# A charge for two narrow token-attention steps in a row in a list schedule, with new priorities, in a macaron layer on one core

## What is computed

```python
x = x + 0.5 * ffn(layernorm(x), ...)
x = x + attn(layernorm(x), ...)
x = x + 0.5 * ffn(layernorm(x), ...)

def ffn(x, ...):                      # per token
    h = rmsnorm(x, gamma1)
    q = (h @ Wq + bq).reshape(b, t, 16, 16)
    kv = ((h @ Wdown + bdown) @ Wup + bup).reshape(b, t, 16, 32)
    k, v = split(kv, 2)
    att = softmax(einsum('bthd,btgd->bthg', q, k) / 4)   # over the heads of ONE token
    out = einsum('bthg,btgd->bthd', att, v).reshape(b, t, 256)
    x = x + (out @ Wo + bo)
    h2 = rmsnorm(x, gamma2)
    gate = softmax(h2 @ Wg + bg)                         # 8 experts
    return x + einsum('btd,edf,bte->btf', h2, We, gate)

def attn(x, ...):                     # 8 groups of 32 features
    scores = einsum('bngh,bmgh->bnmg', q, k) / 16
    probs = softmax(scores, axis=-1)  # over the groups g
    return einsum('bnmg,bmgh->bngh', probs, v)
```

## Time and profile before

| | |
|---|---|
| Median of 3 runs | 992.51 us (992.35 to 993.81) |
| Profiled execution | 993.92 us, span 991.8 us, 28114 instructions |
| PE busy | 953.0 us (96%) |
| PEld busy | 755.2 us (76%) |
| DVE busy | 854.7 us (86%) |
| POOL busy | 792.7 us (80%) |
| ACT busy | 642.2 us (65%) |
| Granted TensorE clock | 1.000 over the span |

### The profile page before, as it was taken

How to read it: one execution, slowest core, us unless ns; L and a number is a source line. 1 busy time by engine, 2 the same in 40 slices (tenths; PEclk the granted TensorE clock), 3 DMA queues, 4 the chain that set the end, 5 groups by cost and what they waited for, 6 DMA issues and landing times. The chain is left out here.

```text
span 991.8 us, 28114 instructions
## 1 busy us (share of the span) xinstructions
PE 953.0 (96%) x11052; PEld 755.2 (76%) x11052; DVE 854.7 (86%) x1388; ACT 642.2 (65%) x1287; POOL 792.7 (80%) x865
## 2 busy tenths in 40 slices
PE   8799999999999989999999999887999999999998
PEld 7678887888888866666666666456788888888886
DVE  6889999899785469999999999999998998898743
ACT  4677566565755467777877877776765765666542
POOL 6988887986885538999899999998778959968554
PEclk9999999999999999999999999999999999999999
DMA  7021000000000000000000000000000000000001
GB/s 226 3 76 45 2 2 2 2 2 2 2 1 1 1 1 2 2 2 2 1 2 2 2 1 2 2 1 2 2 2 22 23 3 22 2 24 22 2 23 42
DMA packets 8398, 14.45 MB, mean 15 GB/s; under 512 B 1993, under 2 KB 5964, under 8 KB 8270
## 3 DMA queue, kind: packets, MB, share of 16 engines
q1 hardware_dynamic: 8270, 12.67, 3.8%
HBM read 8.48 MB, written 4.19 MB: 13 GB/s over the span
## 5 line engine op out<-in xcount | busy, mean ns | idle before, releaser
L514 PE MATMUL psum<-we,h 128*128 128x512 f32 x1536 | 382.2, 399 | 1.6 <-DVE h L1219 1.6
L514 PEld LDWEIGHTS psum<-we,h 128*128 128x128 f32 x1536 | 280.9, 188 | 62.4 <-issue 1.7
L1422 ACT ACTIVATE late<-psum,gate 128x256 f32<-128x256 f32 x252 | 105.0, 469 | 104.2 <-PE psum L514 59.7
L1256 DVE SCALAR_TENSOR_TENSOR X<-psum,gate,X 128x256 f32<-128x256 f32 x260 | 124.0, 477 | 55.9 <-PE psum L514 42.1
L1282 DVE TENSOR_REDUCE oT<-psum 128x128 fp32r<-128x1024 f32 x128 | 154.9, 1218 | 12.9 <-PE psum L914 12.6
L1485 ACT ACTIVATE kvx<-psum 128x1024 f32<-128x1024 f32 x126 | 129.0, 1024 | 52.8 <-PE psum L924 42.2
L997 POOL TENSOR_TENSOR late<-kvx,late 128x2048 f32<-128x2048 f32 x31 | 121.5, 3920 | 35.5 <-ACT late L1492 24.8
L1288 DVE TENSOR_REDUCE late<-kvx 128x256 f32<-128x2048 f32 x63 | 143.4, 2276 | 0.0
L1645 POOL TENSOR_TENSOR late<-late 128x512 f32<-128x512 f32 x63 | 81.4, 1292 | 59.8 <-ACT late L1422 59.6
L997 POOL TENSOR_TENSOR kvx<-kvx,late 128x2048 f32<-128x2048 f32 x31 | 121.4, 3916 | 1.5 <-ACT late L1492 0.8
L1370 ACT ACTIVATE kvx<-kvcs,mask 128x512 f32<-128x512 f32 x132 | 89.5, 740 | 14.8 <-DVE kvcs L1131 8.5
(11 more groups left out here) (185 smaller groups left out, 1935.4 us busy)
## 6 DMA issues: line engine op xcount, KB each, us to landing
X<-in_L_attn_hidden_states SPq DMA_DIRECT2D x7, 512.0 KB, 6.0
out<-X SPq DMA_DIRECT2D x7, 512.0 KB, 2.6
X<-in_L_ffn_We SPq DMA_DIRECT2D x2, 1024.0 KB, 10.5
X<-in_L_attn_hidden_states SPq DMA_DIRECT2D x2, 256.0 KB, 2.9
out<-X SPq DMA_DIRECT2D x1, 384.0 KB, 2.3
late<-in_L_ffn_turned SPq DMA_DIRECT2D x1, 257.0 KB, 4.7
kvx<-in_L_ffn_Wq SPq DMA_DIRECT2D x1, 256.0 KB, 2.8
kvx<-in_L_ffn_Wup SPq DMA_DIRECT2D x2, 128.0 KB, 2.6
```

The costliest lines, as they stand in the source:

```text
L514: ins = e.matmul(out_ap, l, r, start=(n == 0), stop=(n == len(terms) - 1))
L1256: e.scalar_tensor_tensor(out=xi, in0=psum[:, u % 3, w * D:(w + 1) * D], scalar=gate[k % 2][:, i, 2 * n + w:2 * n + w + 1], in1=xi, op0=ALU ...
L1422: e.activation(y[:, n // 2 * 2 + w, :], psum[:, u % 3, w * D:(w + 1) * D], ACT.Copy, scale=gate[k % 2][:, i, 2 * n + w:2 * n + w + 1]).the ...
```

## The change

It adds the entry ("columns", "columns"): 500 to CHANGE, so that in the planned clock a step in columns that follows a step in columns ends 500 ns later. It replaces all values of SOONER and FIRST, and SAME goes from -12780 to 1635. Steps, instructions, durations in the plan, buffers and ATTENTION are the same. What differs in the program is the order of the steps on the four planned engines and which PSUM bank a step takes. The whole diff:

```diff
--- before.py
+++ after.py
@@ -276,32 +276,31 @@
 
 ARRAY = {"score": "rows", "values": "columns", "scores": "columns", "attend": "columns"}
 CHANGE = {("whole", "rows"): 230, ("rows", "whole"): 170, ("rows", "rows"): 280, ("rows", "columns"): 136, ("columns", "rows"): 200,
-          ("whole", "columns"): 140, ("columns", "whole"): 100}
+          ("whole", "columns"): 140, ("columns", "whole"): 100, ("columns", "columns"): 500}
 
 
 def array(step):
 
     return ARRAY.get(step[0], "whole")
 
-SOONER = {"key_A": 401506, "at_zero": 345096, "tokens": 316100, "gate_fold": 308394, "exp": 262595, "mask": 236826,
-          "x1": 229189, "h2T": 207677, "a_exp": 174997, "gate_last": 158516, "wo": 156832, "gate_out": 155627,
-          "normalise": 139058, "one_v": 135085, "score": 130340, "rms2": 128585, "ysum": 126238, "q_zero": 126177,
-          "add": 119096, "split_lo": 101028, "q_turn": 90447, "key_P": 85120, "v": 82622, "h2_lo": 82500, "oT": 77892,
-          "a_back": 76344, "gate_soft": 76146, "out_turn": 70708, "a_hT_hi": 69014, "half": 67157, "finish": 64521,
-          "val_P": 64373, "y": 64124, "we_lo": 58873, "oT_hi": 54906, "hT": 54721, "scores": 52979, "gate_sub": 52176,
-          "attend": 52175, "load": 45816, "val": 44723, "blank": 36588, "hT_hi": 30714, "h2_hi": 30703, "la_one": 26093,
-          "v_bias": 22057, "q": 20437, "split_hi": 18280, "down": 16949, "columns": 15049, "gate_row": 10571, "gate_log": 9524,
-          "norm": 8378, "xs": 8115, "la_v": 7203, "key": 6332, "max": 2252, "norm_first": -585, "inverse": -2047,
-          "a_xs": -8586, "a_total": -18213, "gate_exp": -35498, "val_A": -35857, "la_lo": -36583, "rest_lo": -42422,
-          "rows": -52190, "oT_lo": -54739, "shift": -57432, "x1_base": -60356, "la_hi": -65084, "part": -70643,
-          "expert": -74723, "at": -75388, "mult": -77502, "top": -79510, "qk": -92913, "key_turn": -101463, "xs2": -105384,
-          "a_add": -106124, "hT_lo": -109629, "square": -123106, "spread": -124704, "values": -128120, "turned": -128601,
-          "a_hT": -128870, "norm_outer": -130745, "q_up": -136626, "ct": -155070, "gate_wo": -162710, "fold": -169441,
-          "a_hT_lo": -177314, "last": -201717, "val_turn": -202090, "a_stats": -207977, "v_out": -257634, "x1_norm": -259624,
-          "stats": -266521, "a_rstd": -270978}
-
-FIRST = {0: 22566, 1: 48044, 2: 21974, 3: 22641, 4: -2645, 5: -29335, 6: -2913, 7: 47195}
-SAME = -12780
+SOONER = {"gate_row": 272577, "finish": 258613, "key_P": 257732, "v_bias": 249361, "h2_hi": 248570, "max": 246730,
+          "tokens": 245394, "x1": 228498, "a_back": 215082, "h2_lo": 213513, "a_total": 188846, "oT": 187783, "exp": 180499,
+          "add": 174699, "v_out": 173776, "out_turn": 165270, "y": 162178, "half": 157419, "load": 141307, "la_v": 137715,
+          "hT": 128669, "part": 128498, "q_turn": 126075, "norm_first": 112736, "xs2": 104730, "one_v": 102609, "val": 98228,
+          "attend": 93358, "ct": 92202, "down": 89489, "last": 88662, "gate_fold": 82816, "oT_hi": 81656, "oT_lo": 80447,
+          "gate_soft": 80320, "rms2": 71478, "q_up": 69594, "a_hT_lo": 64997, "norm_outer": 61798, "at": 60028, "key_A": 59712,
+          "gate_last": 57910, "la_one": 57301, "scores": 52632, "h2T": 51395, "rows": 44496, "hT_hi": 40951, "split_hi": 40069,
+          "v": 39472, "a_rstd": 37567, "gate_log": 29410, "shift": 26559, "mult": 23941, "blank": 23837, "a_xs": 19195,
+          "q": 16902, "key_turn": 16687, "wo": 13869, "top": 10350, "key": 10000, "xs": 4124, "square": 1436, "fold": -1205,
+          "val_P": -1326, "ysum": -1765, "gate_exp": -7637, "split_lo": -23046, "hT_lo": -23474, "a_add": -25773,
+          "gate_sub": -29928, "inverse": -34902, "we_lo": -35960, "la_hi": -38971, "at_zero": -39705, "q_zero": -42002,
+          "mask": -46043, "values": -57235, "expert": -72333, "gate_wo": -87151, "a_hT_hi": -89128, "val_turn": -89341,
+          "a_stats": -110628, "norm": -115365, "a_exp": -117924, "normalise": -146987, "columns": -147973, "val_A": -151271,
+          "qk": -159463, "a_hT": -166337, "la_lo": -173287, "turned": -182751, "gate_out": -185243, "spread": -200803,
+          "x1_norm": -207547, "score": -227109, "x1_base": -228874, "rest_lo": -307743, "stats": -337508}
+
+FIRST = {0: -623, 1: -3245, 2: -1058, 3: -42569, 4: 3756, 5: 7377, 6: 80544, 7: -51667}
+SAME = 1635
 
 
 def all_orders(steps, B, units):
```

## The result

| | before | after |
|---|---|---|
| Median | 992.43 us (4 runs, 992.32 to 993.81) | 997.98 us (4 runs, 997.39 to 999.39) |
| Span of the profiled execution | 991.8 us | 995.6 us |
| PE busy | 953.0 us | 957.8 us |
| Mean granted clock | 1.000 | 0.995 (0.986 to 0.995 over the four runs) |

The ratio is 1.0051 with an interval of 1.0039 to 1.0063. The forecast was 990.0 us with a range of 985 to 997.

A forecast was written before the change was run, and what follows sets the result against it. The prediction took TensorE as the bound, busy 953.0 of 991.8 us. Parting narrow steps was to give -2.5 us and the new priorities 0, so 992.5 - 2.5 = 990.0 us, range 985 to 997.

The forecast's parts named there:

- What bounds the kernel: Whole kernel: TensorE busy 953.0 of 991.8 us; 28 us idle in the start, attention's entry and end.
- Gaps as waits for instructions: Runs of adjacent narrow steps (scores, attend): six PE stops, 6.82 us together, read as waiting for the next instructions.
- What a parting costs: Narrow neighbours on PE: putting wide work between two costs 0.33 us for changes of the array's shape.
- How many are parted: Runs of narrow steps: which neighbours the charge parts; cases from -3.9 to +2.6 us, -2.5 taken.
- all 17 parted: All narrow neighbours on PE separated: -6.82 + 17 x 0.33 = -1.2 us.
- the best case: Only the six runs of narrow steps with gaps parted, 9 neighbours: -3.9 us.
- Priorities anew: Start, attention's entry and end: reordering by new SOONER and FIRST, bounds -4 to +4 us, taken as 0.
- rival 2: End of the attention: a 3.6 us feed-forward step on DVE or POOL delays its chain; 994.7 us, chance 0.28.
- The argument for zero: Chain to the second block's first expert product: higher h2_lo gains 1.3 us, against falling attention priorities.
- The sum: Whole kernel: -2.5 for partings plus 0 for priorities, 992.5 - 2.5 = 990.0 us.
- What would show it: PE timeline: neighbours below 8, gaps below 2 us, first-block idle 1 or less; attention-end rival: later expert product, idle 17 or more.
- wrong in its kind: Test of the prediction: gaps at isolated narrow steps, or time moving over 5 us with the ends unchanged.

The follow-up runs named there:

- E1: Not a run: a landmark of PE in every trace, the start of the first expert product; at 52.10 us before, 51.37 us after.
- h_AB: Order of the changed kernel up to the end of the large attention, order of the kernel before from there on; 992.02 us, ratio to before 0.9992.
- h_BA: Order of the kernel before up to the end of the large attention, order of the changed kernel from there on; 1000.56 us, ratio to before 1.0079.
- hT_later: Changed kernel with transposes hT of job 9 moved behind attend 16 on PE, and hT_lo behind mult 16 on DVE; 996.05 us, ratio to before 1.0035.
- E2: Not a run: a landmark of PE in every trace, the start of the first expert product of the second block; 702.52 us before, 704.61 us after.
- before_again: The kernel before, unchanged, run for a second trace; 993.06 us in one run, beside 993.51 for before.

## Why the prediction was wrong, step by step

- *What bounds the kernel.* Right: PE is the engine of both blocks, and idle time is found at the ends. The start moved by 0.7 us, and PE's busy time from 377 to 600 us by 0.1 (221.59 and 221.68).
- *Gaps as waits for instructions.* Right in kind as far as this profile can show it, by the shift of 31 and 32 matmuls. Wrong in its size: I took 6.82 us from one execution as what the gaps cost. That execution was 1.4 us above the median of its kernel, and a second trace has 2.41 instead of 4.86 us between E1 and 320 us. The first block therefore gained 1.0 us (h_AB against h_BA) or 2.8 (the two first traces), not more. The gap of the second block (0.99) did go, but a wait of 1.03 for an operand came in the new order, so nothing was won by it there.
- *What a parting costs.* Mis-sized: 0.33 was read from whole pieces of the chain; moved by hand it is 0.44 of PE's time, and where the later narrow step holds up VectorE another 0.4 to 1.1 us of waiting. In the new order, where the other queues were planned with it, the second block pays 2.7 / 8 = 0.34 a parting, the number of the prediction, but the first pays 0.11. So 0.33 lies inside a range of 0.11 to 0.44, and that it was hit in one block is in part luck.
- *How many are parted.* The sum listed "all 17 parted" with -1.2 us, and this is what came: 0 neighbours. I took -2.5, the middle between it and the best case. Measured, the term is -2.8 to -1.0 in the first block and +2.7 in the second, that is -0.1 to +1.7: the gaps were smaller in the later traces of this order, and parting the eight runs without a gap could save nothing.
- *Priorities anew: 0 between -4 and +4.* This is the step that failed. The end of the attention cost 4.6 us, beyond the upper bound. It is rival 2 that happened, in its place and near to its mechanism: a feed-forward instruction of 3.35 us, the first of norm 9 on POOL, stretched while VectorE did the last normalise. What PE lost by it, however, came through PE's own list, where hT of job 9 stood ahead of attend 16; the half of 4.6 that hT_later gave back is shown, the cause of the other half stays open. I had priced one stretched instruction at 3.6 us, and gave the rival 0.28. The argument for zero, that a higher h2_lo would take statistics off the chain, was half of a comparison: it looked at the steps that gained priority on the chain to E2, not at those of the next job that gained too (hT 55 to 129 thousand, down 17 to 89).
- *The sum.* First block -1 to -2.8, end of the attention +4.6, second block +2.7 give +4.5 to +6.3; the medians differ by 5.5.
- *What would show it.* Neighbours below 8 (0), gaps below 2 us (1.2, with the operand wait of 1.03) and idle time of 1 us or less in the first block (0.95) all came true although the time went the other way: they are signs of the partings, not of a gain. Of rival 2's signs E2 came later (704.61 against 702.52), but the idle time in the two stretches was 15.8 us (13.4 before), less than the 17 given. The prediction also said that it is wrong in its kind if gaps appear at isolated narrow steps. One "issue" wait does stand there (752.09), but it ends with the transposes of its operand, so it doesn't speak against the reading of the gaps.

## What to carry to other kernels

A stop seen in one execution of an order has a price only over several executions. And a change to a planner's cost model is a change of the whole order: price it by the places where the bound engine has nothing else to do, since there a misplaced step can become a wait at once, and not by the places that the new cost is about. Cut the traces at landmarks that all orders share, and compare hybrids of the two orders first: here one pair of runs put the loss behind the attention.

## What the runs showed of the hardware

- TensorE's gaps in dense runs of small matmuls sit at fixed places of its instruction stream. 32 more matmuls at the start moved two of them by 31 and 32 matmuls; at the same place the size went from 1.02 to 0.46 and from 1.23 to 0.77 us between executions, and one of 1.46 was gone. Two other waits marked "issue", of 1.03 and 1.83 us ahead of an attend, ended 0.1 us behind the VectorE transposes of its operand.
- A POOL instruction on 128 x 4 elements took 3.35 us instead of 0.2 while VectorE ran a product of two tiles in SBUF for 3.68 us, and ended with it.
- The granted clock of PE fell for parts of the attention's end (0.67 and 0.69 over 5 us) in the kernel after, in which PE had waited 1.91, 1.59 and 2.92 us there; an attend took 2.04 instead of 1.15 us. In hT_later it stayed at 1.00 over the same steps, with waits of 1.84, 3.11 and 1.83 us, and in before_again, with the old order, it fell too (0.78 and 0.79 from 676 to 684 us). So neither the waits nor the order alone decide it.
